# Attention probabilities as one f32 tile in two column tiles of TensorE, with a new plan of the forty slots

## What is computed

```python
x = x + _layernorm(_L0_attn_ref(_layernorm(x), ...))   # Mamba, both directions
x = x + _layernorm(_L0_ffn_ref(_layernorm(x), ...))    # what follows
# in _L0_ffn_ref, NH = 16 heads, NKV = 4, HD = 8, E = 8 experts, top 2, FFN = 256
h = _rmsnorm(x, ln1_w);  q, k, v = split(h @ wqkv.T)   # rope on q and k
probs = jax.nn.softmax(scores, axis=-1)                # causal
attn = jnp.einsum('bhqk,bkhd->bqhd', probs, v).reshape(B, S, NH * HD)
x = x + jnp.einsum('bso,ho->bsh', attn, wo)
h = _rmsnorm(x, ln2_w);  topw, topi = jax.lax.top_k(softmax(h @ gate_w.T), 2)
out = sum over experts of (silu(h @ w1.T) * (h @ w3.T)) @ w2.T, weighted
return x + out
```

## Time and profile before

| | us |
|---|---|
| median of 3 runs | 2045.14 |
| the profiled execution, its own time | 2054.69 |
| its span, first to last instruction | 2052.8 |
| second phase, from about 1059 in the span | 994 |
| one full period (all five batches in flight) | 108.1 to 109.4 |

### The profile page before, as it was taken

How to read it: one execution, slowest core, us unless ns; L and a number is a source line. 1 busy time by engine, 2 the same in 40 slices (tenths; PEclk the granted TensorE clock), 3 DMA queues, 4 the chain that set the end, 5 groups by cost and what they waited for, 6 DMA issues and landing times. The chain is left out here.

```text
span 2052.8 us, 28868 instructions
## 1 busy us (share of the span) xinstructions
PE 1401.5 (68%) x8048; PEld 986.7 (48%) x8048; DVE 1617.2 (79%) x2570; ACT 1134.1 (55%) x1901; POOL 1380.8 (67%) x1225
## 2 busy tenths in 40 slices
PE   3776666775767767567635877787777787878553
PEld 1444444454534545445422444555555555656453
DVE  2999999999999999999924567586868686866432
ACT  4555665555656545666301877666565666667110
POOL 1776777777777766777742777768686867778333
PEclk9777778887778877778555898899989988999776
DMA  4201222202122102222011112435343524343453
GB/s 161 88 30 55 103 83 103 83 19 85 83 103 83 77 26 83 103 83 98 1 43 43 38 47 79 129 94 153 95 125 97 146 93 139 102 135 117 123 165 93
DMA packets 113886, 184.93 MB, mean 90 GB/s; under 512 B 9856, under 2 KB 86656, under 8 KB 109440
## 3 DMA queue, kind: packets, MB, share of 16 engines
q1 hardware_dynamic: 109664, 175.14, 25.2%
q0 software_dynamic: 4096, 8.40, 1.4%
HBM read 153.03 MB, written 25.89 MB: 87 GB/s over the span
## 5 line engine op out<-in xcount | busy, mean ns | idle before, releaser
L731 POOL TENSOR_TENSOR hc<-hb,cb 128x512 f32<-128x512 f32 x512 | 654.7, 1297 | 247.7 <-DVE hb L610 213.9
L610 DVE TENSOR_TENSOR_SCAN hb<-da,dbu 128x512 f32<-128x512 f32 x512 | 599.9, 1203 | 5.6 <-DVE stats L635 4.0
L499 ACT ACTIVATE da<-dt,a_neg 128x512 f32<-128x512 f32 x512 | 352.2, 718 | 354.8 <-DVE hb L610 303.7
L2041 POOL TENSOR_TENSOR pp<-pt,pp 128x512 f16<-128x512 f32 x320 | 379.0, 1188 | 169.3 <-ACT pt L1550 167.1
L331 PE MATMUL yp<-ident,hc 128*128 128x128 f32 x2048 | 357.9, 317 | 64.9 <-POOL hc L731 64.4
L1689 DVE TENSOR_REDUCE mx<-ms 128x1 f32<-128x384 f32 (+3 forms) x352 | 220.2, 636 | 206.3 <-PE ms L1273 199.4
L331 PEld LDWEIGHTS yp<-ident,hc 128*128 128x128 f32 x2048 | 297.3, 165 | 174.5 <-POOL hc L731 93.9
L603 DVE TENSOR_TENSOR dbu<-dtu,bp 128x512 f32<-128x512 f32 x512 | 324.0, 678 | 2.9 <-PE bp L319 2.2
L1549 ACT ACTIVATE pp<-scores,lift 128x512 f16<-128x512 f32 x320 | 220.3, 688 | 133.4 <-PE scores L1309 128.8
L319 PE MATMUL bp<-st,sel 96*128 96x512 bf16 x256 | 116.7, 456 | 154.3 <-DVE dbu L603 151.7
L1550 ACT ACTIVATE pt<-scores,lift 128x512 f32<-128x512 f32 x320 | 220.3, 688 | 0.0
(11 more groups left out here) (193 smaller groups left out, 2351.8 us busy)
## 6 DMA issues: line engine op xcount, KB each, us to landing
cb<-c_scratch SPq DMA_DIRECT2D x16, 3072.0 KB, 11.9
wt<-ffn_w_e SPq DMA_DIRECT2D x120, 384.0 KB, 3.9
cb<-c_scratch SPq DMA_DIRECT2D x16, 1024.0 KB, 4.6
q<-q_scratch SPq DMA_DIRECT2D x96, 96.0 KB
xg<-xs_scratch SPq DMA_DIRECT2D x8, 960.0 KB, 5.6
ys_scratch<-ysb SPq DMA_DIRECT2D x24, 256.0 KB, 2.3
q_scratch<-qp SPq DMA_DIRECT2D x24, 128.0 KB
k<-k_scratch SPq DMA_DIRECT2D x32, 72.0 KB
```

The lines of the kernel that those rows point to most:

```text
L499: nc.scalar.activation(da[:, s % NDA, :], dt[:, d, h, :], ACT.Exp, scale=a_neg[:, d, h, n:n + 1]).then_inc(da_done, 1)
L610: nc.vector.tensor_tensor_scan(hb[:, s % NHB, :], da[:, s % NDA, :], dbu[:, s % 2, :], 0.0, ALU.mult, ALU.add).then_inc(scan_done, 1)
L731: nc.gpsimd.tensor_tensor(hc[:, s % NHC, :], hb[:, s % NHB, :], cb[:, d, s // 2, :], ALU.mult).then_inc(hc_done, 1)
L2041: nc.gpsimd.tensor_tensor(pp[:, (ST_TILES * b + t) % NPR, 1, 0:width], pt[:, (ST_TILES * b + t) % NPR, 0:width], pp[:, (ST_TILES * b + t) ...
```

## The change

- **P times V.** The f16 exponential and the GpSimd subtraction go. The one f32 exponential `pt` is multiplied by `vpad` in f32: 64 columns, 32 of V and 32 with the ones. Even heads run in the column tile at 0, odd heads in that at 64 (`tile_position`), into disjoint partitions of the bank `og`. `PAIR_TILES` is reordered so that an even and an odd tile of the same width follow each other, and `pe_pv` takes two tiles at a time and alternates between the heads: three calls a pair (`PV_AT`).
- **V.** `act_v` writes one f32 copy, `act_vpad` spreads one part instead of three; `act_vbk` and `pool_v` go. `act_den` copies rows 64 to 128 of `og`, `dve_og` adds rows 0 to 32 and 32 to 64.
- **The plan.** The experts' steps come 4 slots later. The gate moves by about two slots, and most steps of norm, rope, output and end move. `sp_xg` and the first `sp_w` move from the end of a period to the start of the next; `sp_xa` and `sp_h0` move ahead of the third and the second `sp_parts_in`. The projection of V moves to slot 1 of the next period.

```diff
-PAIR_TILES = (((0, 0, 0),), ((0, 1, 0), (0, 3, 384)), ((0, 2, 0), (1, 2, 256)), ((1, 0, 0),), ((1, 1, 0), (1, 3, 384)))
+PAIR_TILES = (((0, 0, 0),), ((1, 0, 0),), ((0, 1, 0), (0, 3, 384)), ((1, 1, 0), (1, 3, 384)), ((0, 2, 0), (1, 2, 256)))
-LAG = 4
+PV_AT = ((4, (0, 1)), (6, (2, 3)), (7, (4,)))
...
-    at = (b - 3, MOE_STEPS - 1) if t == 0 else (b - 2, t // 2 - 1)
+    at = (b - 2, t // 2 - 3) if t >= 6 else (b - 3, MOE_STEPS - 3 + t // 2)
...
-        for f, at in ((0, 10 * q + 9), (1, 10 * q + 13)):
+        for f, at in ((0, 10 * q + 13), (1, 10 * q + 17)):
...
+def pv_at(b, t):
+    for i in range(PAIRS):
+        for late, js in PV_AT:
+            at = NPT * i + late + (i % 2 == 0 and late == PV_AT[0][0])
+            found = b - at // ST_TILES
+            if t == at % ST_TILES and valid(found):
+                yield found, i, js
...
-        vpad = sb("vpad", [P, TC, NHEAD, P], BF16)
+        vpad = sb("vpad", [P, TC, NHEAD, VCOL])
-        pp = sb("pp", [P, NPR, 2, SEQ], F16)
...
             if valid(att):
                 sp_parts_in(sp, att, 3)
+            if valid(moe):
+                sp_xg(sp, moe)
...
+            if valid(moe):
+                sp_w(sp, moe, 0)
             if valid(att + 1):
                 sp_parts_out(sp, att + 1)
             if valid(moe):
                 sp_w(sp, moe, 1)
+            if valid(end):
+                sp_y(sp, end, 3)
...
+            if valid(moe):
+                sp_w(sp, moe, 2)
+                sp_y(sp, moe, 0)
+            if valid(front):
+                sp_h0(sp, front)
             if valid(att + 1):
                 sp_parts_in(sp, att + 1, 1)
             if valid(moe):
+                sp_w(sp, moe, 3)
                 sp_y(sp, moe, 1)
+            if valid(front + 1):
+                sp_xa(sp, front + 1)
...
+        def pe_pv(pe, b, i, js):
+            last_tile = NPT * i + js[-1]
+            pe.wait_ge(exp_done, count(exp_done, b, last_tile + 1))
...
+            for k, (t, h, kc, at) in enumerate(order):
+                col_tile = VCOL * (h % 2)
+                last = nc.tensor.matmul(og[col_tile:col_tile + VCOL, kc * P:], vpad[:, kc, h, :],
+                                        pt[:, (ST_TILES * b + t) % NPR, at:at + SEQ - kc * P],
+                                        start=opens, stop=closes and k >= len(order) - 2,
+                                        skip_group_check=True, tile_position=(0, col_tile))
+            last.then_inc(pv_done, len(js))
...
-            for part in range(3):
-                v_all = vbk[:, part, :, g, :].unsqueeze(2).to_broadcast([P, TC, GH, HD])
-                nc.scalar.activation(vpad_group(32 * part, g), v_all, ACT.Copy).then_inc(vpad_done, 1)
+            v_all = vk[:, :, g, :].unsqueeze(2).to_broadcast([P, TC, GH, HD])
+            nc.scalar.activation(vpad_group(0, g), v_all, ACT.Copy).then_inc(vpad_done, 1)
...
-            nc.scalar.activation(pp[:, (ST_TILES * b + t) % NPR, 0, 0:width], scores_in, ACT.Exp, bias=lift[:, :], scale=SCALE)
             nc.scalar.activation(pt[:, (ST_TILES * b + t) % NPR, 0:width], scores_in, ACT.Exp, bias=lift[:, :],
...
-                    if t == 24:
+                    if t == 18:
                         dve_in(dve, front, 2)
...
-                if valid(att):
-                    pool_split(pool, att, t)
...
-                    if 6 <= t < 6 + TC * TOP:
-                        pool_gather(pool, end, t - 6)
+                    if 11 <= t < 11 + TC * TOP:
+                        pool_gather(pool, end, t - 11)
...
-                    if 31 <= t < 31 + TC * TOP:
-                        pool_scatter(pool, post, t - 31)
+                    if 32 <= t < 32 + TC * TOP:
+                        pool_scatter(pool, post, t - 32)
```

More of the change, by code:

```diff
@@ L1312, in pe_st @@
             last.then_inc(st_ready, 1)
-        def pe_pv(pe, b, t):
-            pe.wait_ge(split_done, count(split_done, b, t + 1))
-            if t % GROUP_TILES == 0:
-                group = t // GROUP_TILES
-                pe.wait_ge(vpad_done, count(vpad_done, b, 3 * (group + 1)))
+        def pe_pv(pe, b, i, js):
+            last_tile = NPT * i + js[-1]
+            pe.wait_ge(exp_done, count(exp_done, b, last_tile + 1))
+            group = i // 2
+            opens, closes = i % 2 == 0 and js[0] == 0, i % 2 == 1 and js[-1] == NPT - 1
+            if opens:
+                pe.wait_ge(vpad_done, count(vpad_done, b, group + 1))
                 pe.wait_ge(og_add, count(og_add, b, 2 * group))
                 pe.wait_ge(den_done, count(den_done, b, 2 * group))
-            ps = pieces(t)
-            for i, (h, kc, at) in enumerate(ps):
-                for part in range(2):
-                    first = t % GROUP_TILES == 0 and part == 0
-                    final = t % GROUP_TILES == GROUP_TILES - 1 and i == len(ps) - 1 and part == 1
-                    last = nc.tensor.matmul(og[:, kc * P:], vpad[:, kc, h, :],
-                                            pp[:, (ST_TILES * b + t) % NPR, part, at:at + SEQ - kc * P],
-                                            start=first, stop=final, skip_group_check=True)
-            last.then_inc(pv_done, 1)
+            tiles_of = [[(t, h, kc, at) for h, kc, at in pieces(t)] for t in (NPT * i + j for j in js)]
+            order = ([p for both in zip(*tiles_of) for p in both] if len(tiles_of) == 2 else tiles_of[0])
+            for k, (t, h, kc, at) in enumerate(order):
[5 more added lines that the diff above has]
+            last.then_inc(pv_done, len(js))
         def pe_wo(pe, b):
@@ L1335, in pe_wo @@
             if valid(b + 2):
[L1336 removed]
+                pe.wait_ge(v_done, count(v_done, b + 2, 1))
             elif valid(b + 1):
@@ L1456, in pe_period @@
                     pe_down(pe, *step)
-                if t < LAG:
-                    if valid(post):
-                        pe_pv(pe, post, ST_TILES - LAG + t)
-                elif valid(att) and (t - LAG) % GROUP_TILES != 0:
-                    if (t - LAG) % GROUP_TILES == 1:
-                        pe_pv(pe, att, t - LAG - 1)
-                    pe_pv(pe, att, t - LAG)
+                for step in pv_at(b, t):
+                    pe_pv(pe, *step)
         @block.tensor
```

257 lines of the change are left out of this document (105 added, 152 removed).

## The result

The changed kernel takes 2025.51 us (median of 4 runs, 2021.13 to 2029.25) where the kernel before, on the same chip, takes 2046.02 (4 runs). The ratio is 0.9886, 95% interval 0.9844 to 0.9928: faster by 1.1%, some 23 us on the 2045.14 of the forecast, where 56 were forecast. A point in what follows is one hundredth of the time of before, 20.5 us; runs taken at different hours are compared by their ratio to the kernel before on the same chip. The 95% intervals reach 0.2 to 0.5 points to either side, so two runs less than half a point apart are not told apart.

A forecast was written before the change was run, and what follows sets the result against it. No engine was full; streams waited for each other slot by slot. Full periods (-26 us together) and periods 0, 1, 2, 6, 7 (-4, -12, -2, -4, -8) gave -56, from 2054.7 to 1998.7, as a median 1989; range 1940 to 2060, own range 1970 to 2010.

The forecast's parts named there:

- GpSimd and ScalarE: Engine load in a full period: GpSimd falls to about 33 us, ScalarE to 43, VectorE from 79.6 to about 69.
- P times V: On TensorE, f32 in two column tiles: 24.7 us a period plus 5.9 for visits, in place of 17.2.
- The order of records that I assumed: In TensorE's P times V, records start in order and wait only for their own tile; an isolated pair takes three records, not four.
- the lower bound: P times V on TensorE if both heads always stream together: 17.4 us a period, against 35 one after another.
- the price of a visit: TensorE going into and out of 64 columns: about 0.24 us a visit, 24 visits a batch, 5.9 us.
- 6.2 us of total for a us of work: Each microsecond of P times V on TensorE is worth 6.2 us in the kernel's total time.
- The waits: TensorE's idle waits in a full period: 10 us kept of 25.1, with tokens, `ga`, exponential and splitting waits cut.
- Half clock and tails, 6: TensorE's half-clock stretches and tails behind waits in a full period: 6 us in place of 14.
- Start and drain together 0: Start of the periods and final drain: no net change together, bounds -8 and +8 us, 4 us allowed at the start.
- the 100 us forecast for a full period: Full period: 84 us of TensorE work, 6 of half clock and tails, 10 of waits, in place of 108.7.
- Both tiles stream together: Rival on P times V: 17.4 us in place of 24.7, full period 94 to 95, total 1942 us; chance 0.20.
- The loads become the bound: Rival: late q and k loads make three groups wait 2 us each, +6 us in seven periods, total 2031; chance 0.18.

The follow-up runs named there:

- e8: Changed kernel with GpSimd's subtraction of each tile put back into a buffer that no product reads; 1.0162 of the kernel before.
- e13: Kernel before with the new P times V alone (old plan), plus GpSimd's subtraction put back into an unread buffer; 0.9846 of the kernel before.
- e7: Changed kernel with ScalarE's second exponential of each tile put back into a buffer that nobody reads; 0.9874 of the kernel before.
- e4: Changed kernel with both ScalarE's f16 exponential and GpSimd's subtraction put back, their output unread; 1.0229 of the kernel before.
- e17: Kernel before with the new f32 P times V in the old plan, but over all 128 columns, head after head; 0.9897 of the kernel before.
- e10: Changed kernel with two buffers for q and k and earlier loads, plus added TensorE products with zero weights; 0.9773 of the kernel before.
- e3: Changed kernel without column tiles: f32 P times V over all 128 columns, head after head; 1.003 of the kernel before.
- e1: Changed kernel with q and k in two buffers by batch parity, each load issued one place earlier on SyncE; 0.9608 of the kernel before.
- e12: Changed kernel with only the chain that makes q and k put back into its old slots; 0.9735 of the kernel before.
- e5: Kernel before with the new P times V and its tile order alone, all other steps in the old plan; 1967.35 us, 0.9562 of the kernel before.
- e2: Changed kernel with only SyncE's order changed: loads of q and k issued ahead of the experts' weights; 0.9814 of the kernel before.
- e16: Changed kernel with the q and k chain in its old slots and q and k in two buffers; 0.9559 of the kernel before.
- e14: Kernel before with the new plan of slots and SyncE order alone, P times V as before; 1.0347 of the kernel before.

## Why the prediction was wrong

The direction was right and the range of 1940 to 2060 held the time, but the forecast's own 1970 to 2010 did not: 2021.8 (0.9886 x 2045.14) for 1989. By its steps:

- *GpSimd and ScalarE.* Right: 32.1 and 44.5 us in period 4 (33 and 43 forecast), VectorE 70.1 (69). That GpSimd's relief is the main gain is shown: its subtraction is worth 2.8 points in either plan (e8, e13), of 4.4 to 4.6 for the whole new P times V. ScalarE's exponential is worth nothing alone (e7) and 0.7 on top of the subtraction (e4). What gives the rest is not taken apart. Of the single instructions, `h` took 424 ns (350 forecast), but `hn` 1014 (528 before): the new plan puts it beside GpSimd's last steps, `yo`. The chain that ended last passes through it:

```profile
1551.40 3.82 DVE L1632 TENSOR_SCALAR hn<-xa,mv,ln_r 128x128 f32<-128x128 f32 x4
1551.38 1.04 POOL L2002 TENSOR_TENSOR yo<-ye,mv 128x512 f32<-128x512 f32 x1
1552.50 1.04 POOL L2005 TENSOR_TENSOR yo<-yo,rt 128x512 f32<-128x512 f32 x1
1553.62 1.26 POOL L2009 TENSOR_TENSOR yo<-yo,xr 128x512 f32<-128x512 f32 x1
```

- *P times V.* Too high: 30.6 us with the visits, 23.6 measured. The order of records that I assumed was wrong; the lower bound was right, and so was the price of a visit (0.25 for 0.24).
- *6.2 us of total for a us of work.* Right only in the old plan, where TensorE is nearly always busy: 6.1 (e17); 3.6 with two buffers in the new plan (e10), 2.6 in the changed kernel (e3). So the 7 us too many in P times V were some 18 us of error and not 43.
- *The waits.* This is the step that failed: 10 us in a full period forecast, 17.0 in period 4. The 10 was too low even by its own terms: 25.1 less 3.1, 4.0, 3.1, 3 and 1.9 is 10.0, and the 4 us for VectorE's late slots come on top of that, 14. `xg` and the exponential went as said, and `ga` (0.6 left). k was given 1.5 and took 8.3; timely loads are worth 2.8 points (e1). The wait for the rotation in slot 35, 1.5 in the same period of before and not in my sum, became 2.8: the moved rope, projections and splits of q and k I had costed at nothing, and they cost 1.5 points (e12). Why VectorE's steps are late in slot 35 I did not follow further.
- *Half clock and tails, 6.* 84.4 busy less 76.6 of work (70.5 - 17.2 + 23.3) is 7.8, and more in periods 0, 2 and 6 (clock 0.83 to 0.91): these periods lost 5 us in sum where I had -10.
- *Start and drain together 0.* Right in sum: +6.0 and -5.7. For the start 4 us were allowed, to SyncE's new order, and it took 6. That the order did it is not shown: the first exponential is at 1129.3 in e5 (old plan), 1136.0 in e2, 1131.8 in e16 and 1126.0 in e1, and e16 and e1 keep the new places of `sp_xa` and `sp_h0`.

In the full periods two errors met: P times V was 7 us too high and the waits 7 too low, so that the 100 us forecast for a full period stand beside 101.3 in period 4. That is luck and not a reading. The 28 us by which the profiled runs fall short of the forecast lie in the full periods (9, nearly all in the two others, 105.0 and 103.1), in periods 0, 2 and 6 (15 in sum) and in period 7 (5); period 1 did 2 better.

In hindsight the answer was two rivals at once. "Both tiles stream together" gave 1942. "The loads become the bound" had the mechanism and put 2 us on each of three groups; it was 2.8. Adding its 42 us and the 31 of the q and k chain to 1942 gives 2015, an estimate made after the fact: e1 puts the loads at 57 us, and the two remedies share some 20. I had treated the plan as neutral and asked of each move only which wait it takes away. One number shows the size of this: the new P·V alone gives 90 us, which I had in the rival (103), and the plan takes 66 of them back.

## What to carry to other kernels

A change that has two halves is measured as four corners; here one half gave 4.4 points and the other cost 3.2, and no view of the combined kernel says so. A moved step is costed by who waits for its end: the steps that feed a single-buffered load, and the load's own start, had less slack than their busy time shows. The price of work on a busy engine is not a constant: look whether waits and a low clock beside it will take it in before multiplying.

## What was new about the hardware

- Two f32 products in column tiles of 64 overlap in full: four records of 512 columns in 1.01 us, the two heads' starts 7 ns apart, both records of each product included. The instructions on `og` are busy 23.6 us in period 4 of the changed kernel (23.1 in e5) and 39.0 in the whole-array form of e17. Of TensorE's whole busy time the difference is 11.3 us, since at the ends of a call they overlap their neighbours:

```profile
1486.80:1589.00 102.20, 39.03 (x128) 0.98 0.42 126
```

- In the changed kernel a wait of 3.58 us was followed by 4 us at a mean granted clock of 0.57 (shown above), which cost half as much again as the wait. In the sums over eight periods the busy time of the same matmuls differs by more (28 us between the changed kernel at 0.91 and e5 at 0.96) than the idle time does (21 us). The other way round, with work added to TensorE the mean clock rose (0.91 to 0.95 in e3, 0.94 to 0.97 in e10), and this paid for a part of it.
- GpSimd's elementwise work on 128x512 tiles stretches VectorE's `h` and `hn` of the same moment: 914 ns for 342 in e13, 1014 in the changed kernel, up to 1420 for a single one beside `yo`. A gather on GpSimd did not: in the changed kernel three `h` beside `yk` took 332 to 334 ns, and the one beside `h2n` 699. Nor did GpSimd's `rt`, 128x4: four `h` beside it took 336 to 356 ns in e14.
